# Attention rounds of a cross-attention and expert kernel: output projection in step 2, query products in step 3

## The reference, cut to what matters

```
xn   = layernorm(x[j])
q    = xn @ w_q.T + b_q ; k, v = ctx[j] @ w_k.T + b_k, ctx[j] @ w_v.T + b_v      # ctx: 77 rows
att  = softmax(q k.T / 4) v            # 16 heads of 16
x2   = x[j] + att @ w_o.T + b_o
p    = softmax(layernorm(x2) @ router_w)        # 8 experts, the best 2 count
out  = x2 + sum over the 2 experts e of p[e] * (silu(x2n @ gate_w[e]) * (x2n @ up_w[e])) @ down_w[e]
```

## Time and profile before

| | |
|---|---|
| median of 3 timed runs | 917.03 us (916.41 to 917.05) |
| the profiled execution | 910.35 us |
| its span, first to last instruction | 908.5 us |
| TensorE's mean granted clock | 0.985 of full speed |
| TensorE, VectorE, ScalarE, POOL busy | 843.3, 588.6, 479.8, 342.4 us |

### The profile page before, as it was taken

The page is one execution under the profiler, slowest core; times in us unless marked ns, Lnnn a source line. Parts: engine busy times, 40 slices in busy tenths (PEclk is TensorE's granted clock), DMA queues, the critical chain, the costliest instruction groups (busy, mean ns, idle before and its releaser), DMA issues.

```text
span 908.5 us, 32045 instructions
## 1 busy us (share of the span) xinstructions
PE 843.3 (93%) x11936; PEld 770.9 (85%) x11936; DVE 588.6 (65%) x1757; ACT 479.8 (53%) x900; POOL 342.4 (38%) x637
## 2 busy tenths in 40 slices
PE   4889899899999987799999999999999999999995
PEld 3677777777777776699999999999999999999995
DVE  6789788788888756566466457446646648544442
ACT  5777777788887774444354335324424435333331
POOL 4789566655666555241122221222222122222112
PEclk9999999999999989899999999999999999999999
DMA  6211322222222543495355228225525632223221
GB/s 211 88 46 45 95 76 66 80 79 68 84 82 66 110 147 119 93 201 132 50 99 122 29 55 174 36 39 108 118 30 99 135 60 36 35 29 32 35 35 18
DMA packets 109876, 74.04 MB, mean 81 GB/s; under 512 B 66444, under 2 KB 99802, under 8 KB 109818
## 3 DMA queue, kind: packets, MB, share of 16 engines
q1 hardware_dynamic: 83898, 36.09, 16.9%
q0 software_dynamic: 13536, 19.85, 12.3%
q10 hardware_dynamic: 12384, 17.35, 7.5%
HBM read 36.27 MB, written 26.80 MB: 69 GB/s over the span
## 4 chain that ended last, share of the span: by engine, by line
PE 75%; issue 5%; ACT 4%; DVE 4%; POOL 1%; DMA 1%; another core or an unknown queue 1%; ACTq 0%; SPq 0%; DVEq 0%; POOLq 0%
PE bank L630 16%; PE bank L632 16%; PE bank L631 16%; PE bank L825 6%; PE bank L827 6%; PE bank L826 6%; PE bank L699 3%; PE bank L706 3%; ACT probs L938 1%; ACT pt_hi L944 1%; DMA raw_tail<-expert_rows 1%; DVE xt_lo L1155 1%; PE bank L755 1%; ACT xt_hi L925 1%
## 5 line engine op out<-in xcount | busy, mean ns | idle before, releaser
L630 PE MATMUL bank<-xg,e_hi 128*128 128x128 f16 x2176 | 374.6, 220 | 5.2 <-issue 3.4
L632 PE MATMUL bank<-xg,e_lo 128*128 128x128 f16 x2176 | 374.6, 220 | 0.5 <-issue 0.5
L631 PE MATMUL bank<-xg,e_hi 128*128 128x128 f16 x2176 | 374.6, 220 | 0.0
L1702 POOL DMA_INDIRECT out<-y_sb,tok_row x67 | 108.4, 1618 | 425.8 <-DVE y_sb L1456 404.2
L630 PEld LDWEIGHTS bank<-xg,e_hi 128*128 128x128 f16 x2176 | 214.0, 98 | 7.2 <-issue 3.1
L631 PEld LDWEIGHTS bank<-xg,e_hi 128*128 128x128 f16 x2176 | 214.0, 98 | 2.8 <-issue 1.2
L632 PEld LDWEIGHTS bank<-xg,e_lo 128*128 128x128 f16 x2176 | 214.0, 98 | 0.0
L1008 ACT ACTIVATE g_act<-bank 128x512 f32<-128x512 f32 x136 | 81.2, 597 | 223.0 <-PE bank L632 207.1
L1461 DVE SCALAR_TENSOR_TENSOR h_full<-bank,g_act 128x512 f32<-128x512 f32 x136 | 94.0, 691 | 121.7 <-ACT g_act L1008 120.7
L825 PE MATMUL bank<-e_hi,h_hi 128*128 128x256 f16 x544 | 148.9, 274 | 4.5 <-DVE h_lo L1467 3.1
L827 PE MATMUL bank<-e_hi,h_lo 128*128 128x256 f16 x544 | 148.8, 274 | 0.9 <-issue 0.8
(11 more groups left out here) (193 smaller groups left out, 1685.8 us busy)
## 6 DMA issues: line engine op xcount, KB each, us to landing
e_stage<-in_gate_w ACTq DMA_DIRECT2D x24, 256.0 KB
e_stage<-in_up_w ACTq DMA_DIRECT2D x22, 256.0 KB
e_stage<-in_down_w ACTq DMA_DIRECT2D x20, 256.0 KB
expert_rows<-pads SPq DMA_DIRECT2D x8, 530.0 KB
xin<-in_x SPq DMA_DIRECT2D x16, 256.0 KB, 3.0
xres<-in_x SPq DMA_DIRECT2D x16, 256.0 KB
out<-x SPq DMA_DIRECT2D x16, 256.0 KB
k_diag<-k_parts SPq DMA_DIRECT2D x124, 9.6 KB
```

What stands on the lines that cost most here:

```text
L630: pe.matmul(dst, a_hi(c), b_hi(c), start=c == 0, stop=False)
L631: pe.matmul(dst, a_hi(c), b_lo(c), start=False, stop=False)
L632: mm = pe.matmul(dst, a_lo(c), b_hi(c), start=False, stop=ends and c == chunks - 1)
L1702: pool.indirect_dma_start(out, bass.IndirectOffsetOnAxis(tok_from[:], 0), y_from[:], None, compute_op=ALU.add).then_inc(added, 16)
```

## The change

The output projection of c and the query product of a change places, and what leads to them goes along.

- TensorE: step 1 turns the attention before x; step 2 issues `project_o`, step 3 `project_q`.
- ScalarE: step 1 copies the attention's high half before x's; `split_q` goes from step 3 to step 4, ahead of `copy_x2`. For the first batch it stays in step 3.
- VectorE: `low_att` goes to the inner list of step 2, ahead of the shift, and `low_x` to the outer list, behind it. `residual` goes from step 4 to step 3 (outer). `low_q` goes from the outer list of step 4 to the inner list of step 5, ahead of that step's shift.

Nothing else differs; the numbers of instructions, transfers and semaphores are the same.

```diff
--- before.py
+++ after.py
@@ -780,9 +780,9 @@
 
             def body(n, a, b, c, r, z):
                 extra = {0: [(z, ranks)],
-                         1: [(not is_first(a) and a, turn_x), (c, turn_att)],
-                         2: [(a, project_q)],
-                         3: [(c, project_o)],
+                         1: [(c, turn_att), (not is_first(a) and a, turn_x)],
+                         2: [(c, project_o)],
+                         3: [(a, project_q)],
                          4: [(r, lambda r: turn_x2(r, rows_at(r)))],
                          5: [(r, router)],
                          7: [(n, project_k), (is_first(n) and n, turn_x), (n, project_v)]}
@@ -985,11 +985,11 @@
                 second = a and a.reg is None and a.plus == 1
                 extra = {0: [(a and not second, lambda _: norm(a, 0, xin, xn, xt_turned, 1, xn_ready, m)),
                              (first, lambda _: split_x(a)), (first, lambda _: spread_half())],
-                         1: [(not first and a, split_x), (c, split_att)],
+                         1: [(c, split_att), (not first and a, split_x)],
                          2: [(r, lambda j: norm(j, 1, x2, x2n, row_ready, 2, x2n_ready, m))],
-                         3: [(a, lambda j: split_q(j, j.plus % 2)), (first, lambda _: split_later()), (first, lambda _: clear_keys(1)),
+                         3: [(first, lambda _: split_q(a, a.plus % 2)), (first, lambda _: split_later()), (first, lambda _: clear_keys(1)),
                              (first, lambda _: norm(n, 0, xin, xn, xt_turned, 1, xn_ready, n))],
-                         4: [(r, copy_x2)],
+                         4: [(not first and a, lambda j: split_q(j, j.plus % 2))] + [(r, copy_x2)],
                          7: [(r, router_exp)]}
                 for u in range(UNITS):
                     if (at := unit(c, b, a, u - 1)) and at[1] in LOW_ON_ACT:
@@ -1349,13 +1349,14 @@
                 slots_chain = take_slots(z, z.plus % 2) if z else None
 
 
-                inner = {2: [(a, low_x)],
+                inner = {2: [(c, low_att)],
+                         5: [(a, lambda j: low_q(j, j.plus % 2))],
                          3: [(n, lambda j: sum_x(j, 0, xin, x_in, 16, x_summed)),
                              (r, lambda j: high_rows(j, rows_at(j)))]}
                 outer = {0: [(a, full_kv)],
                          1: [(c, lambda j: normalize(j, 1))],
-                         2: [(c, low_att)],
-                         4: [(c, residual), (a, lambda j: low_q(j, j.plus % 2))],
+                         2: [(a, low_x)],
+                         3: [(c, residual)],
                          5: [(b, lambda j: normalize(j, 0)), (c, lambda j: sum_x(j, 1, x2, x2_ready, 1, x2_summed)),
                              (m, lambda j: gather(j, n, c) if by_pool(n, b) else start(statistics(j, n, c)))],
```

## The result

The changed kernel takes **942.86 us** (median of 4 runs, 942.21 to 944.38), the kernel before 917.04 in the same job (916.41 to 921.15): a recorded ratio of 1.0265, 95% interval 1.0231 to 1.0298 (the medians alone give 1.0282). It is slower, as forecast, by 25.8 us where 18.9 were forecast; 936 was 6.9 too low, and 942.86 lies inside 923 to 950.

What follows compares the result with a forecast made beforehand. A loop of waits through step-1 copies, projections, VectorE's step 5, gather, inverse root and scatter was taken to bound the rounds. 13.5 + 3 + 0.1 + 0.3 + 2, say 19, on 917.03 gave 936 us, range 923 to 950.

Steps and rivals of the forecast that it cites:

- the delay: VectorE step 5: q_lo waits for the later q_hi copies, so unit 6's shift starts 1.74 us late.
- `x2t`'s lateness is covered: Steps 4 and 5: x2t and the router some 0.7 us later, at no cost, since TensorE's next needed copy moves too.
- the 0.4 taken back: Step 1: turned probabilities' signal may precede the second scatter, recovering 0.4 us; +1.35 a round, 13.5 over ten.
- the upper end of 1.74: Steady round: path over gather, inverse root and scatter, +1.74 us if TensorE's signals are held as before.
- the lower end, 0.57: Steady round: path over ScalarE and TensorE, 1.34 us late less ScalarE's 0.77 of standing in step 1, +0.57.
- the 2 us for TensorE's clock: TensorE in the new rounds: two stops within 5 us may lower its clock; 2 us added, between 0 and 18.
- The argument against: Against the clock dropping in most steady rounds: rounds with a 0.87 us stop in step 1 run at 1.00.
- rounds 2 to 5: Early rounds: 0.77 to 1.74 us late each, less up to 2.41 covered in round 5; 3 taken, 0.7 to 7.0.
- Round 16: The normalisation's 1.61 us wait for TensorE covers all but 0.13 of the delay; 0.1 in the sum.
- only the ScalarE path: Rival, chance 0.20: the scatter's hold meets no needed signal, a round costs +0.57, about 926 us.
- The clock drops in most steady rounds: Rival, chance 0.10: TensorE's clock costs ten times 1.8 us on top of 17, 952 us.
- Not slower: Rival, chance 0.07: VectorE makes up 0.6 between the shifts, unit 7's exponential under 0.77 late, 916 to 918 us.

Runs made afterwards that it cites:

- the first experiment: Changed kernel with the two q_hi copies put back in ScalarE's step 3: 919.34 us, 1.0021 of the kernel before.
- the three delays: Kernel before with useless VectorE casts ahead of step 5's shift, useless ScalarE copies ahead of copy_x2, or both: 943.20, 922.27, 942.47 us.
- The two runs with the late shift: Kernel before with five useless VectorE casts ahead of step 5's shift: 943.20 us; with two useless ScalarE copies ahead of copy_x2 as well: 942.47 us.
- the products' run: Changed kernel plus useless TensorE products, three ahead of step 5's router and four at the end of step 6: 934.75 us.
- the late `x2t` alone: Kernel before with only two useless ScalarE copies ahead of copy_x2 in step 4: 922.27 us, ratio 1.0038.
- the late shift alone: Kernel before with only five useless VectorE casts ahead of step 5's shift: 943.20 us, ratio 1.0237.
- the first ten kernels in the table: The kernel before, the changed one, five edits of the changed one and three delays put into the kernel before: medians from 917.04 to 943.20 us.
- the run with products and split: Changed kernel plus seven useless TensorE products a round, and POOL's scatters three before and one behind the inverse root: 925.05 us.
- the low query last: Changed kernel with q_lo moved on VectorE from ahead of step 5's shift to behind that step's gather: 942.81 us.
- the run with the split alone: Changed kernel with POOL's scatters three before and one behind the inverse root, instead of two and two: 940.91 us.

## Why the prediction came out as it did

**Right, nearly to the hundredth: the delay.** `q_lo` stands 2.23 us (2.2 forecast). The shift of unit 6 is 1.75 later (1.74), its exponential 0.77 (0.77), that of unit 7 1.33 (1.34), the gather 1.73 and the inverse root 1.74 (1.74). The copies' cost fell on the queue where the text put it, and the first experiment and the three delays show that the rest of the change counts for no more than the noise. The residual lost its wait, and no gain shows.

**Right, with a condition: `x2t`'s lateness is covered.** It is 0.71 late and TensorE stands 0.79 for it. The two runs with the late shift, without it (22.20) and with it (22.09), show no cost of its own; alone it costs 0.91 a round.

**Wrong in part: the 0.4 taken back.** The step that failed is "their signal may slip out before the second one". At the end of round 12 it didn't: the turning ended 0.53 before the second scatter started and the copy was still made 1.50 behind that start; seven of the ten rounds have such a wait, on ScalarE or VectorE. Rounds 8 and 12, in which the clock held, are 1.72 and 1.62 longer (21.18 against 19.46, 21.15 against 19.53), near the upper end of 1.74, not 1.35. Over ten rounds this is 14.6 (210.12 of the products' run less 195.52) against 13.5. Without the late signal the rounds are 0.43 longer, not far from the lower end, 0.57; that it is the same path is not shown.

**Wrong by a factor of five: the clock.** The term that failed is the 2 us for TensorE's clock. In the ten rounds it is 220.81 less 210.12, 10.7 us. The argument against, that rounds with a stop of 0.87 us in step 1 run at 1.00, took a stop of ScalarE for one of TensorE, whose longest in that round is 0.45:

```profile
221.27 0.41 PE L706 MATMUL bank<-pt_hi,minus 77*77 77x512 f16 x1 [0.45 <-ACT pt_hi L944]
```

The new stops are two, at the router in step 5 and at the score of step 7 (the second stands for unit 7's shift, not for unit 6's, as the text had it). They need not come together: in round 10 the clock fell behind the router's stop alone, the late `x2t` alone brought two falls in ten rounds, and the late shift alone, without the router's stop, brought the clock down to 0.89. But in rounds 7, 8, 12 and 15 both stops are there and the clock stays, and before the change TensorE stood 1.04 and 1.03 us once each, in rounds 9 and 10, at 1.00. Which rounds fall, the runs don't explain; that filling the stops keeps all ten is shown. The rule that I cited from the Trainium skill ("TensorE: Matmul & The Clock Gate", section "Why this matters for your kernels") had the direction, but its row is on longer gaps than any in these ten rounds, a condition that the prediction left out; by it none of them should have cost the clock, so the measurement decides.

**Too small: rounds 2 to 5.** From the first copy of unit 1 to that of round 6 it was 79.56 us and is 85.63 (108.99 less 23.36): 6.1, where I took 3 between 0.7 and 7.0. Round 5 did swallow its delay (22.02 before, 21.64 now): the stop of 2.41 us is gone, with 0.79 for the router and 0.85 for step 7's score in its place, and the clock, which fell to a mean of 0.92 in that round before, is at 1.00. Rounds 2, 3 and 4 lost 1.0, 2.5 and 2.9, the last two more than the 1.74 that I allowed one round. There the clock is part of it: rounds 3 and 4 show a mean of 0.92 and 0.93 where before shows 1.00, which the prediction had only in its 2 us. How much of the loss is clock and how much waits I haven't worked out.

**Round 16** lost 0.12 (0.1 forecast), since the normalisation's wait is gone:

```profile
340.66 0.25 DVE L1209 RECIPROCAL inv_sum<-bank 128x16 f32<-128x16 f32 x1
```

**The sum.** In the profiles it is 14.6 + 10.7 + 6.1 + 0.1 = 31.5 up to round 17, where 18.9 stood, and 2.5 behind it. That last part I don't put to the change: from there to the end the profiles of the first ten kernels in the table take 590.3 to 594.4 us without order. The terms were 12.6 short by the profiles. That the forecast missed by 6.9 only, inside its range, is in part luck: it added its terms to a median, and the profiled execution of before, from which they were read, was 6.7 faster than that. The slower runs of the kernel before show a lower granted clock (926.51 us at 0.970, 909.30 at 0.984), so its median probably holds falls of the clock that its profile hasn't; no trace shows them.

Of the rivals, "only the ScalarE path" comes near the run with products and split (19.98 a round, 925.05 against 926), in which the late signal was taken out by hand. "The clock drops in most steady rounds" was partly true at 0.92. "Not slower" failed at its own point: unit 7's exponential was 1.33 late, not under 0.77.

## What to carry to other kernels

Before moving a copy on an in-order engine, look for its reader: here 0.8 us of ScalarE's work, one step later, stood VectorE still for 2.2 us with a normalisation's chain queued behind it. Where two loops run through the same delay, price the slower one in full. And a few short stops of TensorE can cost nearly as much in clock as in waiting (10.7 us against 14.6 here), so read them from TensorE's own rows, and don't take rounds at 1.00 for proof that such stops are free: here the same stops cost the clock in six rounds of ten.

## What the runs showed that was not expected

- TensorE's signals came late where two scatters stood back to back on POOL: before and changed, copies of unit 1 that stood for one came 1.50 to 1.66 us behind the second one's start and 1.67 to 2.04 behind the end of the turning. With the low query last, it is unit 0's copies that come 1.0 to 1.2 behind the turning in most rounds, 0.85 to 1.74 behind the second one's start, so that start alone doesn't set it. With one scatter there unit 1's wait was gone, at nearly the same lateness of everything else; in the run with the split alone unit 0's copy still came 0.5 to 0.8 behind its turning in four rounds. What in the chip holds the signals was not found.
- In three rounds that followed a fall of the clock (11, 12 and 15) the late signal didn't reach unit 1's copy, so the two losses are not independent.
- Seven useless products a round, 1.84 us of TensorE (0.81 for three, 1.03 for four), made the changed kernel 8.1 us faster. With these edits to the changed kernel, the split alone was worth 2.0 us (940.91), the products alone 8.1 (934.75) and both together 17.8 (925.05 against 942.86).
